# Projecting one third of a gated convolution once instead of three times, its taps moved to two other engines, in a decoder kernel of one core

## What is computed

```python
x = jnp.einsum('bld,de->ble', u, W_in) + b_in          # D -> 3 D
uc = dw_causal_conv(swapaxes(x), short_w, short_b)     # each channel: 3 taps over the tokens
q, k, v = uc[:, :D], uc[:, D:2 * D], uc[:, 2 * D:]     # gate, key, value channels
v = dw_causal_conv(k * v, inner_w, inner_b)            # 4 taps
y = q * v
return jnp.einsum('bld,de->ble', swapaxes(y), W_out) + b_out
# then x = layernorm(x + mixer), attention of 16 heads of 64, twice, layernorms, feed-forwards
```

## Time and profile before

| | |
|---|---|
| median of three executions | 499.02 us |
| the profiled execution | 498.26 us |
| its span, first to last instruction | 496.3 us |
| busy: PE, DVE, ACT, POOL | 95%, 77%, 74%, 53% of the span |
| mean granted clock of TensorE | 0.988 |
| chain that ended last, by engine | PE 74%, DVE 12%, ACT 6%, issue 3%, DMA 2%, POOL 2% |

### The profile page before, as it was taken

How to read it: one execution, slowest core, us unless ns; L and a number is a source line. 1 busy time by engine, 2 the same in 40 slices (tenths; PEclk the granted TensorE clock), 3 DMA queues, 4 the chain that set the end, 5 groups by cost and what they waited for, 6 DMA issues and landing times.

```text
span 496.3 us, 14185 instructions
## 1 busy us (share of the span) xinstructions
PE 473.1 (95%) x4668; PEld 435.2 (88%) x4668; DVE 381.6 (77%) x1831; ACT 367.2 (74%) x1392; POOL 261.5 (53%) x379
## 2 busy tenths in 40 slices
PE   7778999999999999999999999999999999999993
PEld 7778889999999999999999999999999998798872
DVE  3678778898888977887777777777777777647874
ACT  3547887868677788877778887777777776754864
POOL 3455357665565755555545455544444455534553
PEclk9899999999999999999999999999999999999996
DMA  8750000000000005000000000000000000600004
GB/s 230 232 212 1 1 3 1 2 2 2 1 3 1 3 3 126 1 3 1 3 1 2 2 2 1 2 3 1 4 1 3 1 2 2 171 22 1 6 7 106
DMA packets 15688, 14.58 MB, mean 29 GB/s; under 512 B 2816, under 2 KB 13056, under 8 KB 15488
## 3 DMA queue, kind: packets, MB, share of 16 engines
q1 hardware_dynamic: 14048, 13.20, 9.0%
q10 hardware_dynamic: 1568, 0.47, 0.4%
HBM read 12.23 MB, written 1.44 MB: 28 GB/s over the span
## 4 chain that ended last, share of the span: by engine, by line
PE 74%; DVE 12%; ACT 6%; issue 3%; DMA 2%; POOL 2%; SPq 0%; DVEq 0%; ACTq 0%
PE late_bank L595 11%; PE late_bank L547 10%; PE late_bank L564 10%; PE late_bank L579 10%; PE late_bank L72 9%; PE late_bank L74 8%; PE late_bank L73 8%; ACT P L843 3%; DVE P L1119 3%; PE late_bank L290 2%; PE late_bank L604 1%; PE late_bank L624 1%; PE late_bank L626 1%; PE late_bank L625 1%; DMA tap_rows<-in_short_wT 1%
## 5 line engine op out<-in xcount | busy, mean ns | idle before, releaser
L843 ACT ACTIVATE P<-P,at_negmax 128x128 f32<-128x128 f32 x512 | 198.9, 396 | 78.8 <-DVE at_negmax L1119 78.8
L1529 POOL TENSOR_TENSOR P<-P,at_inv 128x512 f32<-128x512 f32 x128 | 136.6, 1078 | 121.9 <-DVE at_inv L1129 121.9
L1145 DVE COPY at_PT<-late_bank 128x512 f32<-128x512 f32 x128 | 87.6, 687 | 35.4 <-PE late_bank L547 35.3
L1119 DVE CUSTOM_DVE_ANT_0 P<-late_bank,maskb 128x128 f32<-128x128 f32 x512 | 110.5, 287 | 2.4 <-PE late_bank L564 2.4
L843 ACT ACTIVATION_READ_ACCUMULATOR P<-P,at_negmax 128x1 f32 x512 | 100.2, 196 | 0.0
L547 PE MATMUL late_bank<-ident,P 128*128 128x128 f32 x512 | 76.3, 273 | 2.0 <-DVE at_negmax L1119 1.0
L547 PEld LDWEIGHTS late_bank<-ident,P 128*128 128x128 f32 x512 | 59.7, 140 | 8.4 <-issue 3.9
L564 PE MATMUL late_bank<-at_k,at_q 64*128 64x128 f32 x1024 | 65.8, 278 | 0.9 <-DVE at_k L1137 0.9
L564 PEld LDWEIGHTS late_bank<-at_k,at_q 64*128 64x128 f32 x1024 | 59.7, 188 | 4.8 <-issue 1.2
L579 PE MATMUL late_bank<-at_PT,V 128*64 128x128 f32 x1024 | 63.0, 276 | 0.0
L579 PEld LDWEIGHTS late_bank<-at_PT,V 128*64 128x64 f32 x1024 | 55.2, 137 | 3.9
(11 more groups left out here) (199 smaller groups left out, 1068.7 us busy)
## 6 DMA issues: line engine op xcount, KB each, us to landing
ctxT_raw<-in_ctxT SPq DMA_DIRECT2D x1, 1024.0 KB, 8.3
out<-xres SPq DMA_DIRECT2D x4, 224.0 KB, 2.5
x<-in_xT SPq DMA_DIRECT2D x1, 768.0 KB, 10.4
xres<-in_x SPq DMA_DIRECT2D x1, 768.0 KB, 14.4
tap_rows<-in_short_wT SPq DMA_DIRECT2D x3, 192.0 KB, 5.1
sa_wq_raw<-in_sa_wq SPq DMA_DIRECT2D x1, 512.0 KB, 7.0
sa_wk_raw<-in_sa_wk SPq DMA_DIRECT2D x1, 512.0 KB, 9.3
sa_wv_raw<-in_sa_wv SPq DMA_DIRECT2D x1, 512.0 KB, 10.8
```

The source lines that it names most:

```text
L843: last = nc.scalar.activation(P[:, n % 2, h, :], P[:, n % 2, h, :], ACT.Exp, scale=-1.0, bias=negmax[:, n % 2, h:h + 1], accum_out=total[: ...
L1119: last = nc.vector.tensor_tensor_reduce(P[:, n % 2, h, :], score_bank(h), k.maskb[:, cols(n)], scale=1.0, scalar=3.0e38, op0=ALU.add, op1= ...
L1145: nc.vector.tensor_copy(PT[:, HQ * g:HQ * g + HQ, :], banks[T_BANK[g % 2]][:].rearrange("p (h l) -> p h l", h=HQ)).then_inc(pt_ok, 1)
L1529: nc.gpsimd.tensor_tensor(tile, tile, inv[:, n % 2, HQ * g:HQ * g + HQ].unsqueeze(2).to_broadcast([128, HQ, 128]), ALU.mult).then_inc(norm ...
```

## The change

For pairs 3 to 7 the gate part is projected with the plain weights only: three matmuls instead of nine. ACT then reads the bank three times, once for each tap, with the tap as scale and the tap's bias; taps 0 and 1 go into two tiles `tapped`, written two and one columns to the right with zeros before them, tap 2 goes into C. POOL adds the two tiles to C after the product of key and value. `gate` no longer corrects edges for these pairs. The plain weights are split into hi and lo on POOL in a new step `gate_weights` between `gate(1)` and `keys_values(2)`. Pairs 0 to 2 and the key and value parts are as before. C and G move to the memory of `ctxT_hi`, which is written only at items 11 and 12.

```diff
+                if c == 0 and m >= FIRST_PAIRS:
+                    pe.wait_ge(gate_lo, 1)
+                    now = np.s_[:, m % 2, :, 2:2 + L]
+                    mm_split(nc, two(c_bank(m, c)), gate_w, np.s_[:, :], xT, now).then_inc(c_mm, 1)
+                    return
                 for j in range(3):
@@ projected (ACT)
+                if c == 0 and m >= FIRST_PAIRS:
+                    act.wait_ge(blank_taps, 2)
+                    wait(act, tapped_ok, 2 * (m - FIRST_PAIRS))
+                    for j in range(2):
+                        nc.scalar.activation(tapped[j][:, :, 2 - j:2 - j + L], two(c_bank(m, c)), ACT.Identity,
+                                             bias=tap_b[:, c, j:j + 1], scale=taps[:, c, j:j + 1])
+                    nc.scalar.activation(C[:, m % 2, c], two(c_bank(m, c)), ACT.Identity, bias=short_b[:, c:c + 1],
+                                         scale=taps[:, c, 2:3]).then_inc(c_ok, 1)
+                    return
@@ maxima (DVE), item 0 only
+                    vec.wait_ge(gate_lo, 1)
@@ keys_values (POOL)
-                pool.wait_ge(fix_ok, 2 * m + 1)
+                pool.wait_ge(fix_ok, m + 1 + min(m, FIRST_PAIRS))
                 wait(pool, g_ok, m)
                 nc.gpsimd.tensor_tensor(KV[:, :, 3:], C[:, m % 2, 1], C[:, m % 2, 2], ALU.mult).then_inc(kv_ok, 1)
+                if m >= FIRST_PAIRS:
+                    for j in range(2):
+                        wait(pool, tapped_ok, 2 * (m - FIRST_PAIRS) + j)
+                        nc.gpsimd.tensor_tensor(C[:, m % 2, 0], C[:, m % 2, 0], tapped[j][:, :, 0:L],
+                                                ALU.add).then_inc(tapped_ok, 1)
+
+            def gate_weights():
+
+                pool.wait_ge(ld_win, 16)
+                nc.gpsimd.tensor_copy(gate_w.hi[:], w_in[:, 0:D]).then_inc(gate_hi, 1)
+                pool.wait_ge(gate_hi, 1)
+                nc.gpsimd.tensor_tensor(gate_w.lo[:], w_in[:, 0:D], f32(gate_w.hi[:]), ALU.subtract).then_inc(gate_lo, 1)
@@ gate (POOL)
-                edges(m, np.s_[0:1])
-                pool.wait_ge(fix_ok, 2 * (m + 1))
+                if m < FIRST_PAIRS:
+                    edges(m, np.s_[0:1])
+                    pool.wait_ge(fix_ok, 2 * (m + 1))
+                else:
+                    pool.wait_ge(tapped_ok, 2 * (m - FIRST_PAIRS + 1))
@@ POOL's order
             nc.gpsimd.memset(k.half_neg[:], -0.5).then_inc(consts_ok, 1)
+            for j in range(2):
+                nc.gpsimd.memset(tapped[j][:], 0.0).then_inc(blank_taps, 1)
...
             gate(1)
+            gate_weights()
             keys_values(2)
```

More of the change, by code:

```diff
@@ L158, in allocate_last, with allocate_projected, allocate_context_high @@
         sb(ctx, "ffrstd", [128, 4, NSEQ]), sb(ctx, "ffshift", [128, 4, NSEQ]), sb(ctx, "ffminus", [128, 3, NSEQ]))
+def allocate_projected(k, early):
+    k.projected_tiles = k.sb(early, "C", [128, 2, 3, PAIR, L]), k.sb(early, "G", [128, PAIR, L])
+def allocate_context_high(k, ctx):
+    k.ctxT.hi = k.sb(ctx, "ctxT_hi", [128, T], F32R)
 def allocate_attention(k, ctx):
@@ L168, in allocate_attention @@
         k.weights[n], k.raw[n] = k.split_over_raw(ctx, n, [128, INNER])
-    k.ctxT, k.raw["ctxT"] = k.split_over_raw(ctx, "ctxT", [128, T])
+    taken = k.taken
+    with ExitStack() as before:
+        k.raw["ctxT"] = k.sb(before, "ctxT_raw", [128, T])
+    k.taken = taken
+    k.ctxT = Split(None, k.sb(ctx, "ctxT_lo", [128, T], F32R))
+    k.overlay(ctx, allocate_projected, allocate_context_high)
     k.wo_sa = sb(ctx, "wo_sa", [128, H // 2, 128])
@@ L218, in allocate_mixer_tiles @@
     tap_b = k.sb(mixer, "tap_b", [128, 3, 3])
+    k.gate_w = k.split(mixer, "gate_w", [128, D])
+    k.tapped = tuple(k.sb(mixer, f"tapped{j}", [128, PAIR, L + 2]) for j in range(2))
     inner = k.sb(mixer, "inner", [128, 4])
     inner_b = k.sb(mixer, "inner_b", [128, 1])
-    C = k.sb(mixer, "C", [128, 2, 3, PAIR, L])
     KV = k.sb(mixer, "KV", [128, PAIR, L + 3])
-    G = k.sb(mixer, "G", [128, PAIR, L])
     yT = k.sb(mixer, "yT", [128, PAIR, L])
@@ L230, in allocate_mixer_tiles @@
     shift1 = k.sb(mixer, "shift1", [128, PAIR])
-    k.mixer_tiles = (w3, xT, w_out, b_out, taps, short_b, b_in, bias, edge, tap_b, inner, inner_b, C, KV, G, yT,
+    k.mixer_tiles = (w3, xT, w_out, b_out, taps, short_b, b_in, bias, edge, tap_b, inner, inner_b, KV, yT,
                      R1, N1, stats1, mv1, rstd1, shift1)
@@ L321, in mixer_and_attentions @@
         X4, res = k.x1, k.xres
-        (w3, xT, w_out, b_out, taps, short_b, b_in, bias, edge, tap_b, inner, inner_b, C, KV, G, yT, R1, N1,
+        (w3, xT, w_out, b_out, taps, short_b, b_in, bias, edge, tap_b, inner, inner_b, KV, yT, R1, N1,
          stats1, mv1, rstd1, shift1) = k.mixer_tiles
+        C, G = k.projected_tiles
         xT_raw, w_in, tap_rows, w3_raw = k.x1, k.w_in, k.tap_rows, k.w3_raw
@@ L351, in mixer_and_attentions @@
         moved, ze_last = k.sems(ctx, "ff", "moved ze_last")
+        gate_hi, gate_lo, tapped_ok, blank_taps = k.sems(ctx, "mx", "gate_hi gate_lo tapped_ok blank_taps")
+        gate_w, tapped = k.gate_w, k.tapped
         block = ctx.enter_context(nc.Block())
```

## The result

The change takes 503.8 us (median of six executions, 502.93 to 504.82), the kernel before, beside it, 498.54 (497.66 to 500.15): ratio 1.0113 [1.0094, 1.0131], 5.3 us more. A second set of executions of both gave 503.2 against 498.51, 1.010 [1.0079, 1.012], 5.0 us more. The forecast was 501.8: slower was right, its size about half of what was measured. The measured value lies inside the range, 0.1 us under its upper end.

A forecast was written before the change was run, and what follows sets the result against it. The prediction took a chain across engines to bound the early stretch and TensorE the late items. Its terms, 0.7 + 1.6 + 1.45 - 1.0 = +2.75 us on the profiled 498.26, gave 501.0, and 501.8 as median; range 498.5 to 503.9.

The forecast's parts named there:

- What bounds the kernel: TensorE sets the pace in late items with mixer work; between 33.90 and 50.24 us a chain hopping between engines does.
- What comes, per pair: Added work in each changed pair: ScalarE's three activations end after 1.50 us, GpSimd's two additions take 1.5 us.
- Step 1: At the start, GpSimd's split of the gate weights delays pair 1's output bias and VectorE's R: +0.7 us.
- Step 2: At pair 3, the gate's bank freed 1.0 us later and GpSimd work slowing VectorE's convolution: +1.6 us.
- Step 3: In item 1, pair 4's additions ahead of the residuals delay ScalarE's N, TensorE and VectorE: +1.45 us.
- Step 4: At pairs 6 and 7, where TensorE is full, saved matmuls gain 0.5 us each: together -1.0 us.
- Sum: Over the whole kernel, the four steps give +2.75 us, reaching the end because the attentions behind are PE-bound.
- rival D: TensorE's clock falls after its longer wait before pair 4's key projection: 1.5 us added, 503.3 us; chance 0.13.
- queues and loads don't move: Across the kernel, DMA queues and loads were taken as unchanged and given no cost.
- A: TensorE limits everywhere, losses at the waits at 25.84, 47.01 and 67.50 vanish: 495.4 to 496.8 us; chance 0.12.
- B: Engines interfere no more than before: start costs 0.1 and pair 3 1.0, total +1.55, 500.6 us; chance 0.20.
- C: Item 1's delay from pair 4's additions is absorbed by reordered VectorE idle pieces: +1.3, 500.3 us; chance 0.05.

The follow-up runs named there:

- clock_kept: The change plus 44 unread 128-column matmuls on TensorE ahead of its wait before pair 4's key projection; 508.24 us, ratio 1.0204.
- sums_later: The change with GpSimd's sums moved: pair 4's behind the residuals of pair 2, pair 3's behind the first normalisations; 502.67 us, ratio 1.0081.
- weights_only: The kernel before with the change's layout and its gate-weight cast and subtraction at the start, every pair projected three times; 499.64 us, ratio 1.0034.
- pair3_only: Against the kernel before: single projection for pair 3 alone, gate weights split behind pair 1's output bias; 500.59 us, ratio 1.0068.
- clock_short: The change plus 11 unread 128-column matmuls on TensorE ahead of its wait before pair 4's key projection; 501.25 us, ratio 1.0066.
- both_later: The change with the gate weights behind pair 1's output bias and pair 4's sums behind the residuals of pair 2; 500.87 us, ratio 1.0059.
- from4_best: The change with pair 3 as before, gate weights behind pair 1's output bias, pair 4's sums behind pair 2's residuals; 498.73 us, ratio 1.0009.
- pair3_clock: pair3_only plus 11 unread 128-column matmuls on TensorE ahead of its wait before pair 4's key projection; 501.15 us, ratio 1.0064.
- from_pair4: The change for pairs 4 to 7 only, pair 3 as in the kernel before; 501.18 us, ratio 1.0057.
- from_pair6: The change for pairs 6 and 7 only, gate weights still split at the start; 498.24 us, ratio 1.0002.
- from6_late: The change for pairs 6 and 7 only, gate weights behind pair 1's output bias; 497.22 us, ratio 0.9983.
- from6_late_again: The kernel of from6_late unaltered, run once more; 497.42 us, ratio 0.999.

## Why the prediction was right or wrong

**What bounds the kernel: right.** Matmuls removed between 34 and 90 us were worth nothing in the end, those in full items were worth three quarters of their time (1.07 of 1.44 us).

**What comes, per pair: right.** ScalarE's three activations took 1.45 us (1.50 forecast), the sums 1.46 (1.5).

**Step 1, +0.7: right in size, not in its detail.** 0.4 to 0.8 us from G to R, 0.56 against before. R came at 25.94, not after 26.3. I had GpSimd's cast pass and VectorE's subtraction hold up GpSimd's own. Here the cast was the one held, from 0.29 to 1.29 us, and GpSimd's subtraction behind it was undisturbed (0.46). As I had it, it went in `clock_kept` and `sums_later`: cast 0.29, GpSimd's subtraction 1.33 and 1.32. By time `weights_only` lost 1.7 [0.8, 2.5], so these lie at its lower end or under it.

**Step 2, +1.6: right in size.** 1.63 in the profile of `pair3_only`, 1.60 in that of `clock_short`; by time `pair3_only` lost more, as said. By the rule in the Trainium skill, "SBUF — State Buffer", "Who interferes with whom", I had 2.2; the trace gave less. The convolution grew by 0.35 us only, and the rest of the contention, 0.3 us, fell on the low part of the next pair's input. But I had both sums fall beside the convolution, and they were over before it began: four operations alternating with VectorE's four did not take place, so these runs don't test that reading of the rule.

**Step 3, +1.45: right for the stall, and pair 5's saving is lost as said.** The stall is 1.43 (`sums_later`) and 1.40 (`both_later`). Pair 5's 0.72 shows up in item 2 and goes in item 3, where PE waits 0.75 for VectorE's maxima: at 85.23, the same transposes that the forecast named at 80.42.

**Step 4, -1.0: right, for another reason.** Net -1.07: each pair gives its full 0.73 and the item behind takes 0.2 back. I had capped it at 0.5 by VectorE.

**Sum: the step that failed is the one that I left out.** The four steps give 2.75; without a fall of the clock at item 1, `clock_short` shows 2.21 us at item 31, with a start that was 0.1 late where I had 0.7. The sum put the clock at nothing, by making it rival D with a chance of 0.13. That was wrong: D's wait grew to 2.71 us as I wrote, and the clock fell in each of the four profiles with such a wait. D's price was 1.5; it measured 1.3 in the change, 1.56 in `from4_best`. A second term was put at nothing without a reason, "queues and loads don't move": in both profiles of the change the load of xE was late, which is 1.8 of the 5.8 us in the first. Whether that is the change's doing is open. Step 2 and D are one event: step 2 makes the wait of 2.7 us that the earlier trace rows had already shown to be long enough, at 2.17. The Trainium skill, "TensorE: Matmul & The Clock Gate", "HAM oscillation — how this bites in real kernels", describes a loop in which TensorE's waits for DMA, longer ones than these, bring the clock down. The trace agrees that a wait does so, here one of 2.6 to 2.7 us for VectorE. I had given it one chance in eight. With D the sum is 4.25 on the forecast's own numbers, 503.3. The rest to 5.0 and 5.3 is within the interval of the second set [3.9, 6.0] and just outside that of the first [4.7, 6.5]. That the range held the measured time is luck in part: its upper end came of steps 1 to 4 all at their worst, and they were not.

**The other rivals.** A is out: all three waits grew. B is out by 1.29 us for the cast and 1.63 for pair 3. C is out by ScalarE's 2.06.

**The median against the profile.** The profiled execution of the change lost 5.8 us of span; 1.8 of it was the load of xE, which `clock_short`, `both_later` and `pair3_clock` don't show (it landed in 2.7, 2.6 and 2.6 us). Item 31 accounts for 3.95 of the 5.0 to 5.3 us that the timed executions lost; the other 1.0 to 1.4 is not assigned. A load that is late in part of the executions would fill it, but no run shows that it does. For the clock the timed executions speak: in the second set the change's mean is 0.0042 under that of before beside it, 2.1 us of the span; one fall as in the windows above makes 1.7. For single kernels profile and time differ in both directions: `from_pair4` is 0.6 us late at item 31 and 2.8 by time, `from_pair6` 1.5 late and 0.1 by time.

## What to carry to other kernels

When an edit lengthens a chain on which TensorE waits, price the length of the wait itself: a wait that grows past the one after which the clock has already been seen to fall costs the delay and then the slow matmuls behind it, and the two belong in one case, not in a case and its rival. Take operations off a bound engine only where it is full (here pairs 6 and 7) and leave the stages alone in which a chain across engines sets the pace; there the helpers' added work goes straight into the time. And compare from mark to mark, over several profiles, with the granted clock of each stretch: where the clock stayed up, the distances of one kernel repeated to 0.05 us. A fall of it made one distance 1.2 us longer between `from6_late` and `from6_late_again`, and the tail moved by 1.2 between the two profiles of before.
